# Layer 1's opening: the first graph's score columns and rows ahead of its values, in banks of their own

## The reference, cut to what matters

```python
h = jnp.maximum(_layernorm(x, axis=-1), 0.0)
x = x + _L1_gnn_ref(h, adj, L1_gnn_W, L1_gnn_a)

def _L1_gnn_ref(x, adj, W, a):
    Wh = jnp.einsum('bnf,hfd->bhnd', x, W)
    a1, a2 = (a[:, :hs], a[:, hs:])
    ei = jnp.einsum('bhnd,hd->bhn', Wh, a1)
    ej = jnp.einsum('bhnd,hd->bhn', Wh, a2)
    e = ei[:, :, :, None] + ej[:, :, None, :]
    e = jnp.where(e > 0, e, ALPHA * e)
    e = jnp.where(adj[None, None] > 0, e, MASK_VAL)
    att = jax.nn.softmax(e, axis=-1)
    h = jnp.einsum('bhij,bhjd->bhid', att, Wh)
    ...
```

## Time and profile before

| what | value |
|---|---|
| median of 3 runs | 2103.32 us (2099.75 to 2114.32) |
| the profiled execution | 2103.01 us, its span 2101.2 us, mean granted TensorE clock 0.908 |
| PE busy | 1671.2 us (80%) |
| DVE busy | 1600.2 us (76%) |
| ACT busy | 1339.1 us (64%) |
| POOL busy | 122.9 us (6%) |
| layer 0 | from 0 to about 735 us |
| layer 1's opening, up to its first head on ACT | 735 to 771.41 us |
| layer 1's first graph with that head | 771.41 to 836 us; a later graph takes 48.3 us |
| layer 3 begins | about 1720 us |

### The profile page before, as it was taken

The page is one execution under the profiler, slowest core; times in us unless marked ns, Lnnn a source line. Parts: engine busy times, 40 slices in busy tenths (PEclk is TensorE's granted clock), DMA queues, the critical chain, the costliest instruction groups (busy, mean ns, idle before and its releaser), DMA issues. The chain is left out here.

```text
span 2101.2 us, 36838 instructions
## 1 busy us (share of the span) xinstructions
PE 1671.2 (80%) x13620; PEld 1065.1 (51%) x13620; DVE 1600.2 (76%) x2710; ACT 1339.1 (64%) x1751; POOL 122.9 (6%) x130
## 2 busy tenths in 40 slices
PE   2888887878788557799989886777877757999997
PEld 1333343334333246677767665556655554455544
DVE  3676877868778745888888899888898856766664
ACT  2665656656655357667777698898888834455453
POOL 0000110100100100000000000000000000000000
PEclk9989989989999858899998998878998879999999
DMA  7545254353453131111111121112111211000000
GB/s 205 134 100 128 70 132 105 91 126 96 98 125 87 51 114 41 41 51 41 41 51 42 42 72 67 57 61 74 62 64 68 73 57 39 11 11 20 10 11 20
DMA packets 74923, 146.51 MB, mean 70 GB/s; under 512 B 11937, under 2 KB 34722, under 8 KB 74754
## 3 DMA queue, kind: packets, MB, share of 16 engines
q1 hardware_dynamic: 74754, 144.23, 24.6%
HBM read 101.85 MB, written 8.78 MB: 53 GB/s over the span
## 5 line engine op out<-in xcount | busy, mean ns | idle before, releaser
L1050 ACT ACTIVATE g<-s_all,steep_d 128x1024 fp8e4<-128x1024 f32 x608 | 642.4, 1135 | 42.9 <-PE acc L991 20.6
L991 PE MATMUL acc<-parts,g 128*128 128x102 bf16 (+1 forms) x6144 | 418.0, 229 | 27.0 <-DVE sums L1141 19.7
L991 PEld LDWEIGHTS acc<-parts,g 128*128 128x128 fp8e4 x6144 | 401.5, 99 | 60.6 <-issue 43.6
L973 PE MATMUL post<-parts,edge 128*128 128x396 bf16 (+1 forms) x1024 | 234.4, 385 | 84.9 <-DVE base L1149 84.9
L561 ACT ACTIVATE e<-s_ps 128x1024 f32<-128x1024 f32 x256 | 248.4, 1023 | 24.9 <-PE s_ps L420 18.6
L1134 DVE TENSOR_TENSOR g<-g,edge 128x1024 int32<-128x1024 int32 x192 | 227.9, 1218 | 32.6 <-ACT g L1050 32.5
L706 DVE SCALAR_TENSOR_TENSOR e<-e,bound 128x1024 f32<-128x1024 f32 x160 | 188.7, 1213 | 32.1 <-ACT e L561 30.9
L416 PE MATMUL s_ps<-qs,ks 128*128 128x512 f32 x512 | 200.3, 502 | 9.5 <-issue 7.6
L973 PEld LDWEIGHTS post<-parts,edge 128*128 128x128 fp8e4 x1024 | 102.5, 103 | 192.8 <-issue 108.7
L432 PE MATMUL sum_ps<-e,pick 128*32 128x256 f32 x2048 | 142.3, 397 | 67.5 <-DVE e L703 39.4
L567 ACT ACTIVATE chunk<-ctx_ps 128x512 f32<-128x512 f32 x128 | 76.3, 596 | 171.0 <-PE ctx_ps L441 171.0
(11 more groups left out here) (152 smaller groups left out, 2149.9 us busy)
## 6 DMA issues: line engine op xcount, KB each, us to landing
s_all<-s_rows SPq DMA_DIRECT2D x96, 512.0 KB, 3.7
inv_all<-inv_rows SPq DMA_DIRECT2D x256, 128.0 KB, 2.8
qs<-split SPq DMA_DIRECT2D x128, 128.0 KB, 3.2
ks<-split SPq DMA_DIRECT2D x128, 128.0 KB, 2.4
x<-in_x SPq DMA_DIRECT2D x8, 512.0 KB, 6.8
inv_rows<-inv SPq DMA_DIRECT2D x32, 128.0 KB, 1.7
adj_in<-in_adj SPq DMA_DIRECT2D x8, 512.0 KB, 4.1
out_x<-x SPq DMA_DIRECT2D x8, 512.0 KB, 3.2
```

Of the source, the lines that this page charges most:

```text
L973: ins = pe.matmul(self.post[:, it % 2, 0:H * 3 * W1].rearrange("p (h k c) -> p h k c", h=H, k=3), self.c.edge[:, jt, it * P:(it + 1) * P], ...
L991: ins = pe.matmul(self.acc[:, bank, o:o + self.NS], self.g[:, h % RING, jt, it * P:(it + 1) * P], self.upper[par][:, jt, h, :, :].rearrang ...
L1050: act.activation(self.g[:, h % RING, jt, :], self.s_all[:, h % 2, :], ACT.Relu, bias=self.steep_d[par][:, jt, h:h + 1], scale=STEEP, satur ...
```

## The change

Graph 0 of layer 1 gets its own opening. `pe_open` runs the columns and the rows straight after `h_t(0)`, before the values, and puts them into `acc`: the columns into bank 2, the rows into banks 0 and 1. They no longer wait for a copy out of `aux`, nor the rows for `sd`. ACT's `act_row_open` copies the rows from `acc` right behind `h_t(0)`, ahead of `wh(0)` and `h(1)`. `dve_sd` takes the columns from `acc`. PE waits for layer 1's weights only ahead of the values, and for layer 2's only after the rows of graph 1. The turn of graph 1 waits for `wh(0)`, the last reader of `aux`. The number of instructions stays.

```diff
+    def pe_open(self, pe):
+
+        c, H = self.c, self.H
+        pe.wait_ge(self.nm.h_t_ready, self.nm.upto(0))
+        for t in range(T):
+            ins = pe.matmul(self.acc[:, 2, t * 2 * H:(t + 1) * 2 * H], c.h_t[:, t * P:(t + 1) * P],
+                            self.wa[:, :, :].rearrange("p k h -> p (k h)"), start=True, stop=True)
+        ins.then_inc(self.sd_projected, 1)
+        for i in range(2):
+            ins = pe.matmul(self.acc[0:H, i, :], self.wa[:, 0, :], c.h_t[:, i * HALF:(i + 1) * HALF], start=True, stop=True)
+        ins.then_inc(self.row_projected, 1)
...
+    def act_row_open(self, act):
+        act.wait_ge(self.row_projected, 1)
+        act.wait_ge(self.row_stored, 16)
+        act.activation(self.s_row, self.acc[0:self.H, 0:2, :].rearrange("p a n -> p (a n)"),
+                       ACT.Copy).then_inc(self.row_ready, 1)
...
-                pe.wait_ge(a.loaded, 16 * a.layer)
 
             def prepare():
-                for n in range(2):
-                    one.pe_turn(pe, n, n)
-                    one.pe_values(pe, n, n)
-                    one.pe_columns(pe, n, n)
-                    one.pe_rows(pe, n, n)
+                one.pe_turn(pe, 0, 0)
+                one.pe_open(pe)
+                pe.wait_ge(one.loaded, 16)
+                one.pe_values(pe, 0, 0)
+                pe.wait_ge(one.wh_ready, 1)
+                one.pe_turn(pe, 1, 1)
+                one.pe_values(pe, 1, 1)
+                one.pe_columns(pe, 1, 1)
+                one.pe_rows(pe, 1, 1)
+                pe.wait_ge(two.loaded, 32)
...
                 one.act_h_t(act, 0, 0)
+                one.act_row_open(act)
                 one.act_wh(act, 0, 0)
                 one.act_h(act, 1, 1)
-                one.act_row(act, 0, 0)
                 one.act_h_t(act, 1, 1)
...
-                one.dve_sd(dve, 0, 0)
+                one.dve_sd(dve, 0, 0, one.acc[:, 2, :])
```

More of the change, by code:

```diff
@@ L1066, in dve_stats, with dve_sd @@
         nm.dve_moments(dve, n)
-    def dve_sd(self, dve, n, par):
+    def dve_sd(self, dve, n, par, source=None):
         sd = self.sd
@@ L1071, in dve_sd @@
         dve.tensor_copy(sd[:, :, :, :].rearrange("p t k h -> p (t k h)"),
-                        self.aux[:, 0:T * 2 * self.H]).then_inc(self.sd_ready, 1)
+                        (self.aux if source is None else source)[:, 0:T * 2 * self.H]).then_inc(self.sd_ready, 1)
         dve.wait_ge(self.sd_ready, n + 1)
```

## The result

| | before | after |
|---|---|---|
| median, runs | 2107.28 us, 6 (2099.75 to 2114.32) | 2095.9 us, 6 (2092.67 to 2098.0) |
| the profiled execution's span | 2101.2 us | 2095.8 us |
| layer 0, up to the issue of layer 1's value weights | 735.60 | 744.65 |
| opening: from there to ACT's first head | 35.81 | 28.95 |
| layer 3 begins (issue of `w_t`) | 1720.06 | 1714.51 |

The ratio is 0.9942, 95% interval 0.9919 to 0.9966, so a gain of 12 us, with 7 to 17 possible. The forecast was 2095.5 us with a gain of 7.5. The change did shorten the opening by 6.86 us. What else sets the two spans apart is not the change: layer 0, whose code is the same, took 9.05 us longer in this execution, and layer 2, the same as well, 8.0 us less between the 9th and the last of POOL's maxima.

The account below looks back on a forecast made before the run. Layer 1's opening was taken as a chain carried by one engine after another, delayed by `w_out`. Gains of 6.1 (chain) and 1.4 (clock) made 7.5 us: 2103.0 − 7.5 = 2095.5 us, range 2087 to 2104.5.

Parts of the forecast that it names:

- The bare loss: Layer 1's opening: PE's turn waits for layer 2's `w_out`, which nothing in layer 1 reads; 5.70 us lost.
- The chain: Layer 1's opening, turn to first head: with every product slow, the head starts at 765.3, a gain of 6.1 us.
- the clock's bounds: Gain from PE's high clock in graph 0's values and graph 1's turn: between 0 and 2.7 us.
- ACT's list: First head on ACT: queued behind `wh(0)`, `h(1)`, `h_t(1)` and exponentials until 765.3, while `s_all` waits since 760.6.
- POOL: First head's exponentials: rival that POOL's maximum doesn't follow `sd` and stays at 767.91; gain 2.5 us, 2100.5 us, chance 0.07.
- The carry: After the first head: PE and DVE keep their distance to ACT, `sd(1)` 7.85 us behind; layer 3 begins as much earlier.
- The clock: PE in graph 0's values and graph 1's turn: a high clock was taken to save about half its bounds, 1.4 us.
- the all-slow chain: Layer 1's opening with every product at its slow, low-clock duration: first head at 765.3, gain 6.1 us.
- The slower rival: PE's later heads: shifted gaps cost clock, 2.2 us per slow group; with six, 2108.5 us; chance 0.10.

Follow-up runs that it names:

- wait_only: Kernel before with PE waiting for layer 1's weights only ahead of the first values, layer 2's after graph 1's rows; old order kept; ratio 0.9970.
- queue_order: Kernel before with layer 2's two weights issued on SP ahead of the eight adjacency tiles; PE's waits and order unchanged; ratio 0.9961.
- h1_early: Kernel after with `h(1)` on ACT moved from behind `wh(0)` to directly behind `h_t(0)`; ratio 0.9950 to the kernel before.
- order_only: Kernel after with the wait for both layers' weights put back at the start of PE's list; ratio 0.9990 to the kernel before.
- the second measurement: Kernel after, unchanged, profiled and timed once more; ratio 0.9954 (0.9936 to 0.9972) to the kernel before.
- warm: Kernel after with 8 extra matmuls of 512 columns, read by nobody, at the start of PE's list; ratio 0.9964 to the kernel before.
- rows_head_warm: Kernel after with 8 extra matmuls, rows ahead of columns, `h(1)` behind `h_t(0)`, three first-head tiles ahead of `h_t(1)`; ratio 1.0001 to the kernel before.

## Why the prediction was right, point by point

**The bare loss.** Forecast 5.70 us from the turn's earlier start; measured 5.56 against the first trace of before, 5.85 against the second. wait_only and queue_order show it alone.

**The chain.** Counted from the issue (735.60), the forecast's turn 8.2, columns 11.3, `s_row` 18.2, issue of `s_all` 21.1; measured 8.31, 11.36, 18.48, 21.35. The rows took 3.58 where I had put 3.30. The head with every product slow was forecast at 29.7 and with half of the clock's bounds at 28.3; measured 28.95 and 27.47. The head was held by ACT's list, as said, and h1_early proved it by moving one group.

**POOL.** From `sd` to the maximum 6.85 us were forecast; 766.69 − 759.63 = 7.06 were measured. That rival fell: the some 6 us lie behind the semaphore and move with it. The Trainium skill ("GPSIMD Engine Reference", 2.1 Instruction dispatch) says that the first call of a newly loaded kernel pays about 6 us for loading its code, behind MODIFY_POOL_CONFIG and with no instruction in the profile; 767.52 − 761.9 = 5.6 us in the earlier trace rows agrees in size. But this is not the program's first all-reduce (layer 0 has one at 48.68 us), and 15 of the 16 in layers 1 and 2 show idle time that no releaser ends; only the second, with nothing of POOL's between it and the first, is released by DVE.

**The carry.** `sd(1)` was forecast 7.85 us behind the head and stands 8.30 behind; the gain at the third maximum is 8.25 us in the mean against 7.8 at the head. Layer 1's later graphs repeat at 47.5 to 49.3 us in both kernels, and at the ninth maximum, near the end of layer 1, the gain is 8.5 us (402.8 and 403.9 before, 396.1 and 393.7 after). Layer 3 was to begin as much earlier as the head. It begins 984.5 and 978.7 us behind the issue before, 969.9 and 971.0 after, which is 11.2 us in the mean; but the two traces of the kernel before alone lie 5.8 us apart there, so how the gain passes through layer 2 is not shown.

**The clock.** The size, 1.4 us, was within what came: the all-slow chain with rows at 3.58 makes 30.0, and the heads stood 1.0 and 2.5 us ahead of that. The values were the place (3.03 and 2.08 us in place of 3.78), in the second trace with 0.5 us from the turn of graph 1 (1.42 us). But one step of the reasoning was wrong: I had taken from the earlier trace rows that values and columns do not bring the clock up. In wait_only and queue_order, with the old order and an earlier start, the columns behind the values ran at the high clock, 1.95 to 1.98 us, in all three traces; in the new order, where they stand ahead of the values, they took 3.58 in all five traces that start at the same 8.3 us. So the new order gives up 1.6 us in the columns for the up to 1.7 us that it gains in the values. Order alone does not decide it: in the kernel before, with the old order and the later start, the columns took 3.58 us in both traces. What does is open.

That is one reason why the reordering is worth only 1.4 us beside the wait, though it issues `s_all` 3.7 us earlier (21.35, and 25.04 in wait_only). The other is the one of the prediction, ACT's list: with every product slow its sum leaves the reordering 6.1 − 5.7 = 0.4 us, and h1_early, which changes that list alone and has its columns at 3.58 too, brought 2.2 us more.

The Trainium skill ("TensorE: Matmul & The Clock Gate", Part 1) says that the moment of the rise varies from run to run. The values of graph 0 bear that out, 3.03 and 2.08 us in two traces of the kernel after, 2.05 and 2.94 in two of order_only; the columns, at 1.95 twice in wait_only and at 3.58 in both traces of before, after and order_only (3.59 once), did not vary within a kernel.

**The sum and the range.** 2095.5 was forecast and 2095.9 measured, and part of that agreement is luck: the sum was made against an execution of 2103.0 us, while the kernel before has medians of 2107.3, 2107.5, 2106.9 and 2107.7 us over 6, 31, 21 and 23 runs. Against that, the measured gain is 11.4 us and the second measurement gives 9.7 (6 to 13.5), where the traces show 8.25. What lies beyond 8.25 is within the intervals, and no trace shows that the change causes it.

**The slower rival.** Its mechanism is real: PE's clock moves single graphs of layer 2 by 3 us and more. But it does so in the kernel before as well, and it took no side.

## What to carry to other kernels

Look first for a wait on something that its engine doesn't need yet: it was worth about 7 of the 8.25 us here, and moving two transfers ahead of 4 MB did it without touching an engine. When a chain is shortened, ask which list holds its end next; here moving one group on ACT brought 2.2 us more in the trace, while getting a later stage started at the expense of the next graph brought nothing. Where executions of unchanged code differ by more than the gain, count times in the trace from a mark just ahead of the change.

## What the runs showed of the hardware

- Layer 0, the same in all kernels, ended between 735.60 and 745.98 us over 14 traces, and a graph of layer 2 took 63.7 to 71.5 us, at granted clocks of 0.82 and 0.89 in the two shown.
- Eight f32 products of 8 columns with 128x128 weights took 3.58 us at 1.2 GHz (granted 0.50) and 1.95 at 2.4 (granted 1.00 in wait_only and warm), about as much as two f32 products of 512 columns (3.58 and 1.88).
- Behind layer 0, standstills of PE that no semaphore explains moved when its list grew: one of 7.2 to 7.6 us at 1455 to 1470 us in the kernels without the extra matmuls; with 8 of them, one of 2.5 to 2.65 us near 993, and none (warm) or one of 3.40 us (rows_head_warm) near 1457.
- In wait_only PE's clock was 1.00 in the columns and 0.50 again from the start of the rows, with 0.32 us of idleness between them, and 1.00 once more in the turn of graph 1.
